# A transformer block on one core: a ring of three PSUM banks for the maxima, two for dense products, a split gelu block, two reciprocal transfers, and a new order of all steps

## What is computed

```python
c_proj = silu(c) @ W_mod + b_mod
shift_a, scale_a, gate_a, shift_m, scale_m, gate_m = split(c_proj, 6)
q, k, v = split(modulate(ln(x), shift_a, scale_a) @ W_qkv + b_qkv, 3)
x = x + gate_a * (softmax(q k^T / 4) v @ W_proj + b_proj)           # self attention
q_c = ln(x) @ W_qc + b_qc
k_c, v_c = split(ln(context) @ W_kvc + b_kvc, 2)
x = x + softmax(q_c k_c^T / 4) v_c @ W_cproj + b_cproj               # cross attention
h = gelu_tanh(modulate(ln(x), shift_m, scale_m) @ W_mlp1 + b_mlp1)
x = x + gate_m * (h @ W_mlp2 + b_mlp2)
```

## Time and profile before

| | |
|---|---|
| Median of three runs | 1634.08 us (1629.98 to 1639.45) |
| The profiled execution | 1633.06 us, span 1631.3 us |
| Mean granted clock of TensorE | 0.958 of full |
| PE busy | 1406.4 us, 86% |
| DVE, ACT, POOL busy | 1145.2 (70%), 1130.6 (69%), 718.4 (44%) |

### The profile page before, as it was taken

How to read it: one execution, slowest core, us unless ns; L and a number is a source line. 1 busy time by engine, 2 the same in 40 slices (tenths; PEclk the granted TensorE clock), 3 DMA queues, 4 the chain that set the end, 5 groups by cost and what they waited for, 6 DMA issues and landing times.

```text
span 1631.3 us, 40543 instructions
## 1 busy us (share of the span) xinstructions
PE 1406.4 (86%) x15090; PEld 918.4 (56%) x15090; DVE 1145.2 (70%) x2477; ACT 1130.6 (69%) x2343; POOL 718.4 (44%) x1005
## 2 busy tenths in 40 slices
PE   3477899989999899999999999999999998988764
PEld 1234466666666666666665666666666566655433
DVE  4657877777887777777788777777778877765411
ACT  3144687877777777787777778777777777776541
POOL 2232345454455445445445544544544544543222
PEclk8678999999999999999999999999999999999877
DMA  5122333233233233233323333323232323321100
GB/s 157 51 74 74 94 92 90 91 89 95 81 97 92 86 89 96 87 90 90 93 86 96 89 90 90 95 90 88 90 99 81 95 85 90 86 74 59 44 28 20
DMA packets 166118, 138.08 MB, mean 85 GB/s; under 512 B 45921, under 2 KB 156674, under 8 KB 165922
## 3 DMA queue, kind: packets, MB, share of 16 engines
q1 hardware_dynamic: 165922, 135.48, 27.9%
HBM read 56.60 MB, written 9.57 MB: 41 GB/s over the span
## 4 chain that ended last, share of the span: by engine, by line
PE 33%; SPq 20%; ACT 20%; DMA 11%; DVE 8%; issue 5%; POOL 3%; POOLq 0%; ACTq 0%; DVEq 0%
SPq L436 12%; PE o_ps L678 8%; SPq L469 6%; ACT G L835 6%; PE dense_ps L351 5%; PE max_ps L643 4%; PE dense_ps L353 4%; PE dense_ps L352 4%; DMA r_dram_cross<-o_r_cross 4%; DMA o_rb_cross<-r_dram_cross 3%; ACT g_split L789 3%; DVE mx_self L1002 3%; PE exp_ps L660 3%; ACT probs L804 3%; PE dense_ps L585 3%
## 5 line engine op out<-in xcount | busy, mean ns | idle before, releaser
L804 ACT ACTIVATE probs<-exp_ps 128x512 f32<-128x512 f32 x1024 | 558.1, 602 | 247.8 <-PE exp_ps L660 244.6
L1002 DVE TENSOR_REDUCE mx_cross<-max_ps 128x2 f32<-128x512 f32 x512 | 328.4, 683 | 202.6 <-PE max_ps L643 198.4
L1002 DVE TENSOR_REDUCE mx_self<-max_ps 128x2 f32<-128x512 f32 x512 | 329.0, 684 | 62.6 <-PE max_ps L643 59.3
L1110 POOL TENSOR_TENSOR o_n_self<-o_n_self,o_rb_self 128x512 f32<-128x512 f32 x32 | 40.6, 1269 | 267.1 <-DMA o_rb_self<-r_dram_self 267.1
L1143 POOL TENSOR_TENSOR g_split<-G,g_split 128x512 f16<-128x512 f32 x128 | 144.7, 1156 | 28.2 <-ACT g_split L789 26.6
L660 PE MATMUL exp_ps<-q_stack_cross,k_stack_cross 50*128 50x256 f16 x1024 | 100.7, 274 | 63.8 <-ACT probs L804 55.4
L351 PE MATMUL dense_ps<-mlp_hi,g_split 128*128 128x256 f16 x512 | 141.9, 277 | 6.4 <-POOL g_split L1143 3.9
L678 PE MATMUL o_ps<-probs,V_cross 128*32 128x256 f32 x2048 | 141.9, 396 | 0.6 <-ACT o_sb_cross L812 0.6
L351 PE MATMUL dense_ps<-xt,mlp_hi 128*128 128x256 f16 x512 | 140.7, 275 | 1.9 <-DVE xt L964 1.9
L678 PE MATMUL o_ps<-probs,V_self 128*32 128x256 f32 x2048 | 142.2, 397 | 0.0
L352 PE MATMUL dense_ps<-mlp_lo,g_split 128*128 128x256 f16 x512 | 140.7, 275 | 0.0
(11 more groups left out here) (212 smaller groups left out, 3351.3 us busy)
## 6 DMA issues: line engine op xcount, KB each, us to landing
q_stack_self<-split_q SPq DMA_DIRECT2D x192, 64.0 KB, 2.6
k_stack_self<-split_k SPq DMA_DIRECT2D x192, 64.0 KB, 2.5
k_stack_cross<-split_kc SPq DMA_DIRECT2D x192, 64.0 KB, 2.6
q_stack_cross<-split_qc SPq DMA_DIRECT2D x192, 64.0 KB, 2.6
X<-in_x SPq DMA_DIRECT2D x32, 256.0 KB, 2.8
Ctx<-in_ctx SPq DMA_DIRECT2D x32, 256.0 KB, 3.0
rows_a<-rows_a_dram SPq DMA_DIRECT2D x32, 256.0 KB, 4.1
o_n_self<-o_sb_self SPq DMA_DIRECT2D x64, 128.0 KB, 3.0
```

The costliest lines, as they stand in the source:

```text
L804: nc.scalar.activation(probs[:, (t + ab) % 8], exp_ps[:, ab], ACT.Exp).then_inc(exp_taken[kind], 1)
L1002: nc.vector.tensor_reduce(mx[kind][:, :, ab, t // 2], max_ps[:, ab].rearrange("p (q k) -> p q k", q=2), AX_X, ALU.max).then_inc(max_taken[ ...
```

## The change

- The maxima get a ring of three banks. A MAX pair waits until all tiles but the last one of the pairs before have been reduced. The dense units have two banks left.
- The gelu block has the four pairs of gelus only. The copies to float16 become four steps `g_hi_0` to `g_hi_3` with slots of their own. A gelu of one element on `gelu_primer` stands ahead of the wait for `mlp1_0`.
- `r_fetch` reads the reciprocals back in two DMAs of 64 partitions instead of eight of 16. `o_sb` and `r_dram` are laid out to fit.
- All steps have new slots, and EXP begins in slot 8 instead of 6. The order is now computed in `Timeline` from absolute slots, with the same lags and the same order in a slot.

```diff
 PLAN = {
-    "load_x": (-1, 0, 0), "ln1": (-1, 0, 4), "norm1": (-1, 0, 6), "t1": (-1, 0, 8), "t1_hi": (-1, 0, 9),
-    "t1_lo": (-1, 0, 10), "q": (-1, 1, 1), "q_hi": (-1, 1, 3), "q_lo": (-1, 1, 4), "stack_q": (-1, 1, 8),
-    "k": (-1, 1, 6), "k_hi": (-1, 1, 6), "k_lo": (-1, 1, 8), "stack_k": (-1, 1, 10), "v": (0, 0, 7),
-    "v_hi": (0, 0, 8), "split_self": (0, 0, 15), "m_self": (0, 1, 0), "m_copy_self": (0, 1, 0),
-    "o_gather_self": (1, 0, 13), "o_recip_self": (1, 0, 13), "r_out_self": (1, 0, 14), "r_back_self": (1, 0, 14),
-    "o_norm_self": (1, 0, 14), "o_hi_self": (1, 1, 4), "o_lo_self": (1, 1, 7), "rows_a": (0, 1, 7),
-    "xr": (0, 1, 12), "proj": (1, 1, 9), "x2": (1, 1, 11), "x2_add": (1, 1, 11), "ln2": (1, 1, 13),
-    "norm2": (1, 1, 14), "t2": (2, 0, 1), "t2_hi": (2, 0, 1), "t2_lo": (2, 0, 2), "qc": (2, 0, 5),
-    "qc_hi": (2, 0, 5), "qc_lo": (2, 0, 6), "stack_qc": (2, 0, 8), "xc": (3, 1, 10), "load_c": (0, 0, 14),
-    "lnc": (0, 0, 15), "normc": (0, 1, 7), "tc": (1, 0, 14), "tc_hi": (1, 0, 14), "tc_lo": (1, 0, 15),
-    "kc": (1, 1, 3), "kc_hi": (1, 1, 7), "kc_lo": (1, 1, 9), "stack_kc": (2, 0, 5), "vc": (2, 0, 10),
-    "vc_hi": (2, 0, 11), "split_cross": (3, 0, 0), "m_cross": (3, 0, 0), "m_copy_cross": (3, 0, 2),
-    "o_gather_cross": (3, 1, 10), "o_recip_cross": (3, 1, 13), "r_out_cross": (3, 1, 13),
-    "r_back_cross": (4, 0, 1), "o_norm_cross": (4, 0, 1), "o_hi_cross": (4, 0, 4), "o_lo_cross": (4, 0, 4),
-    "cproj": (4, 0, 6), "x3": (4, 0, 7), "ln3": (4, 0, 9), "norm3": (4, 0, 12), "rows_b": (3, 1, 4),
-    "t3": (4, 0, 13), "t3_hi": (4, 0, 13), "t3_lo": (4, 0, 14), "xm": (4, 0, 13), "mlp1_0": (4, 1, 0),
-    "mlp1_1": (4, 1, 1), "mlp1_2": (4, 1, 1), "mlp1_3": (4, 1, 1), "gelu": (4, 1, 0), "g_lo_0": (4, 1, 6),
-    "g_lo_1": (4, 1, 6), "g_lo_2": (4, 1, 6), "g_lo_3": (4, 1, 7), "mlp2_0": (4, 1, 10), "mlp2_1": (4, 1, 12),
-    "mlp2_2": (4, 1, 14), "mlp2_3": (5, 0, 2), "y": (5, 0, 4), "y_add": (5, 0, 4), "store": (5, 1, 3),
+    "max_self": (0, 0, 0), "exp_self": (0, 1, 8), "max_cross": (2, 1, 0), "exp_cross": (3, 0, 8),
+    "load_x": (-1, 0, 4), "ln1": (-1, 0, 9), "norm1": (-1, 0, 11), "t1": (-1, 0, 13), "t1_hi": (-1, 0, 13),
+    "t1_lo": (-1, 0, 13), "q": (-1, 0, 15), "q_hi": (-1, 0, 15), "q_lo": (-1, 1, 0), "stack_q": (-1, 1, 6),
+    "k": (-1, 1, 0), "k_hi": (-1, 1, 0), "k_lo": (-1, 1, 5), "stack_k": (-1, 1, 9), "v": (0, 0, 12),
+    "v_hi": (0, 0, 12), "split_self": (0, 1, 0), "m_self": (0, 1, 3), "m_copy_self": (0, 1, 3),
+    "o_gather_self": (1, 0, 11), "o_recip_self": (1, 0, 12), "r_out_self": (1, 0, 13), "r_back_self": (1, 0, 14),
+    "o_norm_self": (1, 1, 6), "o_hi_self": (1, 1, 6), "o_lo_self": (1, 1, 10), "rows_a": (0, 1, 13),
+    "xr": (1, 0, 3), "proj": (1, 1, 13), "x2": (1, 1, 13), "x2_add": (1, 1, 15), "ln2": (1, 1, 15),
+    "norm2": (2, 0, 8), "t2": (2, 0, 8), "t2_hi": (2, 0, 8), "t2_lo": (2, 0, 8), "qc": (2, 0, 11),
+    "qc_hi": (2, 0, 11), "qc_lo": (2, 0, 11), "stack_qc": (2, 0, 12), "xc": (3, 1, 1), "load_c": (0, 1, 1),
+    "lnc": (1, 0, 10), "normc": (1, 1, 1), "tc": (1, 1, 9), "tc_hi": (1, 1, 9), "tc_lo": (1, 1, 9),
+    "kc": (2, 0, 1), "kc_hi": (2, 0, 4), "kc_lo": (2, 0, 7), "stack_kc": (2, 0, 11), "vc": (2, 0, 14),
+    "vc_hi": (2, 0, 15), "split_cross": (2, 1, 15), "m_cross": (2, 1, 15), "m_copy_cross": (3, 0, 1),
+    "o_gather_cross": (3, 1, 10), "o_recip_cross": (3, 1, 14), "r_out_cross": (3, 1, 15),
+    "r_back_cross": (4, 0, 6), "o_norm_cross": (4, 0, 9), "o_hi_cross": (4, 0, 10), "o_lo_cross": (4, 0, 10),
+    "cproj": (4, 0, 13), "x3": (4, 0, 13), "ln3": (4, 0, 13), "norm3": (4, 1, 3), "rows_b": (4, 0, 0),
+    "t3": (4, 1, 4), "t3_hi": (4, 1, 5), "t3_lo": (4, 1, 8), "xm": (5, 0, 11), "mlp1_0": (4, 1, 10),
+    "mlp1_1": (4, 1, 10), "mlp1_2": (4, 1, 10), "mlp1_3": (4, 1, 10), "gelu": (4, 1, 10), "g_hi_0": (4, 1, 10),
+    "g_hi_1": (4, 1, 13), "g_hi_2": (4, 1, 15), "g_hi_3": (5, 0, 1), "g_lo_0": (4, 1, 12), "g_lo_1": (5, 0, 0),
+    "g_lo_2": (5, 0, 1), "g_lo_3": (5, 0, 1), "mlp2_0": (5, 0, 5), "mlp2_1": (5, 0, 8), "mlp2_2": (5, 0, 9),
+    "mlp2_3": (5, 0, 10), "y": (5, 0, 10), "y_add": (5, 0, 12), "store": (5, 1, 14),
 }
 
 BANK = {
-    "m_self": 2, "m_cross": 0, "qc": 2, "cproj": 0, "tc": 0, "kc": 1, "t3": 1, "mlp1_0": 1, "mlp1_1": 0,
-    "mlp1_2": 2, "mlp1_3": 1, "vc": 1, "t1": 0, "proj": 0, "mlp2": 1, "q": 0, "k": 2, "v": 1, "t2": 2,
+    "m_self": 1, "m_cross": 1, "qc": 0, "cproj": 0, "tc": 0, "kc": 0, "t3": 1, "mlp1_0": 0, "mlp1_1": 1,
+    "mlp1_2": 0, "mlp1_3": 1, "vc": 0, "t1": 1, "proj": 0, "mlp2": 1, "q": 1, "k": 0, "v": 1, "t2": 0,
 }
 
-DENSE = {n: BANK[n] for n in sorted(BANK, key=lambda n: PLAN["mlp2_0" if n == "mlp2" else n][1:])}
-MAX_LAG = {"self": 0, "cross": 2}
-EXP_LAG = {"self": 0, "cross": 3}
-EXP_START = 6
+AHEAD = {}
+
+PE_ORDER = ("m_self", "m_cross", "qc", "cproj", "tc", "kc", "t3", "mlp1_0", "mlp1_1", "mlp1_2", "mlp1_3", "vc", "t1",
+            "proj", "mlp2", "q", "k", "v", "t2")
 AV_AFTER = 6
+MAX_BANKS = 3
...
+def moment(step, n):
+    lag, half, slot = PLAN[step]
+    return ((n + lag) * 2 + half) * TILES + slot - AHEAD.get(n, {}).get(step, 0)
+class Timeline:
+    def __init__(self, batches, kinds):
+        self.steps, self.max, self.exp, self.av = {}, {}, {}, {}
+        for n in range(batches):
+            b = Batch(n)
+            for kind in kinds:
+                for t in range(0, TILES, 2):
+                    self.max[moment(f"max_{kind}", n) + t] = (kind, b, t)
+                    self.exp[moment(f"exp_{kind}", n) + t] = (kind, b, t)
+                for g in range(4):
+                    self.av[moment(f"exp_{kind}", n) + AV_AFTER + 4 * g] = (kind, b, g)
+            for step in PLAN:
+                if step[:4] not in ("max_", "exp_"):
+                    self.steps[step, moment(step, n)] = b
+        assert len(self.steps) == batches * (len(PLAN) - 2 * len(kinds))
+        assert len(self.max) == len(self.exp) == batches * len(kinds) * TILES // 2
+        def predecessors(turns):
+            turns = [t[1:] for t in sorted(turns)]
+            return dict(zip(turns[1:], turns))
+        every = [(kind, n) for kind in kinds for n in range(batches)]
+        self.max_before = predecessors((moment(f"max_{k}", n), k, n) for k, n in every)
+        self.max_at = {t[1:]: i for i, t in enumerate(sorted((moment(f"max_{k}", n), k, n) for k, n in every))}
+        self.exp_before = predecessors((moment(f"exp_{k}", n), k, n) for k, n in every)
+        self.tenant_before = {}
+        for bank in set(BANK.values()):
+            self.tenant_before.update({unit[1:]: before[1:] for unit, before in predecessors(
+                (moment("mlp2_0" if u == "mlp2" else u, n), i, u, n)
+                for i, u in enumerate(PE_ORDER) if BANK[u] == bank for n in range(batches)).items()})
+        self.first = min(at for _, at in self.steps)
+        self.last = max(max(at for _, at in self.steps), max(self.av))
...
-        max_ps, exp_ps, o_ps, dense_ps = psum("max_ps", 2), psum("exp_ps", 2), psum("o_ps", 1), psum("dense_ps", 3)
+        max_ps, exp_ps, o_ps, dense_ps = psum("max_ps", MAX_BANKS), psum("exp_ps", 2), psum("o_ps", 1), psum("dense_ps", 2)
...
+        def max_bank(kind, b, tile):
+
+            return (line.max_at[kind, b.n] * TILES + tile) % MAX_BANKS
...
             def r_fetch(b, kind):
                 sp_wait(r_out[kind][b.u], dmas(b, 1))
                 sp_wait(o_mult[kind], b.n)
                 for g in range(2):
-                    for j in range(4):
-                        src = r_dram[kind][b.u, j, :, g]
-                        (i_step, i_n), (e_step, e_n) = [tuple(v) for v in src.ap]
-                        nc.sync.dma_start(o_rb[kind][64 * g + HD * j:64 * g + HD * j + HD],
-                                          bass.AP(tensor=src.tensor, offset=src.offset,
-                                                  ap=[[0, HD], [i_step, i_n], [e_step, e_n]])).then_inc(o_rb_in[kind][b.u], 16)
+                    rows = r_dram[kind][b.u, :, g]
+                    (j_step, j_n), (e_step, e_n) = [tuple(v) for v in rows.ap]
+                    nc.sync.dma_start(o_rb[kind][64 * g:64 * g + 64],
+                                      bass.AP(tensor=rows.tensor, offset=rows.offset,
+                                              ap=[[j_step, j_n], [0, HD], [e_step, e_n]])).then_inc(o_rb_in[kind][b.u], 16)
...
+            def tenant(b, unit):
+
+                if (prev := line.tenant_before.get((unit, b.n))):
+                    pe.wait_ge(taken[prev[0]], prev[1] + 1)
+                return dense_ps[:, BANK[unit]]
+
...
-                    if (prev := previous(it, max_order, MAX_LAG, kind)):
-                        pe.wait_ge(max_taken[prev[0]], prev[1].n * TILES + TILES)
+                    if (prev := line.max_before.get((kind, b.n))):
+                        pe.wait_ge(max_taken[prev[0]], prev[1] * TILES + TILES - 1)
                 else:
```

(31 more changed lines are left out.)

621 lines of the change are left out of this document (277 added, 344 removed).

## The result

The changed kernel takes 1626.59 us (median; 1621.13 to 1633.67) against 1633.69 for the kernel before on the same chip: ratio 0.9958, 95% interval 0.9942 to 0.9974. It is faster by 0.4%, where 2.9% was forecast: inside the range, far from the value. The prediction called anything within 8 us no change and gave it a chance of 0.08.

The account below looks back on a forecast made before the run. TensorE was taken to bound the steady stretch, busy 92%, with ACT and DVE waits; a loop bound the drain. Steady -16, filling -4 and drain -27 sum to -47 us from 1634.08: 1587 us, range 1552 to 1632.

Parts of the forecast that it names:

- filling, first gelu load: Filling: cheaper MAX pairs save 4 us, while the new plan puts gelu 12.8 us later in its iteration.
- steady stretch: 27 iterations between gelu loads 1 and 28: period from 45.4 to 44.8 us, a gain of 16 us.
- loads 28 to 32: Drain: gelu no longer holds up the next batch's exponents, so four iterations take 126 us instead of 167.6.
- end behind it: After the last gelu load: stays near 23 us, with 2 us lost for the last batch, whose copies follow all gelus.
- the ring: PE's waits on maxima banks: 1.0 us gained an iteration; in the filling a MAX pair about 0.6 cheaper, -4 us altogether.
- the landing of the reciprocals: Two wide read-back DMAs: landing taken as 3 us, 4.3 from first issue to POOL's product, covered by the plan.
- rival D: Wide reciprocal transfer or `stack_qc` lands late, blocking ACT and DVE: 1684 us, or 1641 with one late by 2; chance 0.11.
- rival E: The drain's loop stays shut by in-order queues and the steady gain is nil: 1630 us; chance 0.08.
- `mlp1_2` with two dense banks: Dense unit `mlp1_2` must wait for the gelu of unit 0 to free its bank: cost 0.24 us an iteration.
- The wait behind the gelu block: PE waiting for exponents (EXPs6) after the gelu block: 1.8 us an iteration, where it waited 1.6 before.
- New waits of tight exponents: Closely spaced exponents wait for ACT: EXPc14 0.43, EXPs0 0.15, EXPs2 0.61 us, together 1.2 an iteration.
- The prediction's own sign of being wrong: Drain: gelu loads still 40 us apart in the profile after, instead of 29 to 33, would show the forecast wrong.

Follow-up runs that it names:

- e7: e1 with PE waiting for all earlier maxima tiles to be taken, as two banks would force, so the third bank goes unused; 1633.8 us.
- e1: Changed kernel with each reciprocal row read back in a DMA of its own, eight for a head set instead of two; 1600.8 us.
- e3: Changed kernel with four reciprocal DMAs of two rows and 32 partitions instead of two of four rows and 64; 1725.6 us.
- e6: Changed kernel with one reciprocal DMA of eight rows, `r_dram` laid out head set first and denominators gathered in two DMAs; 1601.6 us.
- e4: Changed kernel with the two cross reciprocal DMAs issued earlier, `r_back_cross` at slot (4,0,0) instead of (4,0,6); 1607.4 us.
- e5: Changed kernel with `load_x` moved from right ahead of the cross reciprocal DMA pair to right behind it; 1606.0 us.
- e11: e7 with two banks for the maxima and a third dense bank that `mlp1_2` alone uses; 1625.1 us.
- e10: e1 without the small gelu that loads the gelu table early, ahead of the wait for `mlp1_0`; 1632.2 us.
- e12: e1 with the last copy left in the gelu block, `g_hi_0`, moved behind the first exponents after the block; 1674.8 us.
- e14: e12 with `x2` and `o_recip_cross` placed behind the split of the cross maxima and `ln2` at (2,0,1); 1641.8 us.
- e13: e12 with POOL's subtraction `g_lo_0` moved to (5,0,0), behind `x2_add`; 1630.8 us.
- e9: e1 with copies `g_hi_1` to `g_hi_3` back in the gelu block, ahead of the exponent table's load; 1686.7 us.

## Why the prediction was right or wrong

**Against the profiled execution** (-46.8 forecast, -12.3 measured) the terms stand so:

| term | forecast | measured |
|---|---|---|
| filling, first gelu load (-4, and 12.8 later by plan) | +8.8 | +8.8 |
| steady stretch | -16 | -4.8 |
| loads 28 to 32 | -41.6 | -19.4 |
| end behind it | +2 | +3.1 |

(For the last batch, which needs no load, the start of its first gelu at 1596.13 is taken.)

The first row agrees by luck. By e7 the ring is worth 7.2 us of filling, not 4, so the rest of the plan puts the first load some 16 us later, not 12.8. In the last row the prediction has the end before "near 23"; by the earlier trace rows it is 19.8, and 22.9 after.

**The steady stretch** failed in one term, the landing of the reciprocals. The prediction took a landing of 3 us, so 4.3 from first issue to product; 7.3 is the median (7.87 in the rows shown), a landing of 6. The prediction named the row that was nearest, 3.9 for a broadcast of 256 KB, and the rule that spoke against its 3, and then took a value between the rows, by size; by e1, e3 and e6 size is not what orders the landings. With the landing on time (e1, e4, e5, e6) the period is 44.54 to 44.57; 44.8 was forecast, 16.2 us in 27 iterations, and it would have been 22. (The steady sum leaves out the 0.1 that the prediction had booked for the other dense units.) The point from which rival D decides, a landing of 6 us, was about right: with 7.3 from issue to product the changed kernel loses 0.65 us an iteration, with 6.6 (e5) nothing. Its price, 38 us for one product late by 2, was too high: the cross product is 1.3 us later than in e1, and the profile 20 us longer. So the time lies near that of rival E (1630), but the cause is that of D; the prediction had the mechanism of its loss among its rivals and priced it out of the range.

**Ring, banks, early load.** 1.0 an iteration for the ring: 0.78 by e7, and 7.2 us of filling where 4 was taken. 0.24 for `mlp1_2` with two dense banks: 0.30 by e11. The wait behind the gelu block: 1.8 by start times (1.82 in the sum), 1.56 idle measured, 1.73 by start times (MAX at 1082.12, EXP at 1084.08 in e1, less 0.23). New waits of tight exponents, by start times, 0.43, 0.15 and 0.61: 0.49, 0.24 and 0.53 in e1, of which 0.32, 0 and 0.37 are idle. These steps were right. The gains do not add up, though: without the ring alone (e7) or the early load alone (e10) the whole gain of e1 is gone. No run takes the new order of steps back, so its own share is not known.

**The drain** failed by the size of one iteration. I took 33, 32, 32 and 29 us for the four and measured 42.9, 42.1, 32.8 and 30.4. The pieces of one drain iteration were listed as if it held the cross half alone. Two windows of the changed kernel:

```profile
1448.00:1491.00 43.00, 36.24 (x382) 21.89 (x381) 20.32 (x46) 30.60 (x63) 19.77 (x26) 0.96 0.21 64
1491.00:1533.00 42.00, 33.29 (x300) 21.42 (x301) 20.60 (x42) 21.93 (x45) 14.96 (x19) 0.88 0.16 46
```

PE alone is busy for 36.2 and 33.3 us: between load 28 and 29 the self exponents of the last batch, and up to load 30 most of its cross maxima and the projections for them, are still to be done. Work was missing from the sum, not waits. The prediction's own sign of being wrong, loads still 40 us apart, came for these two. Only the third and fourth are of the kind that was costed. The late transfer adds to it: with eight DMAs the first two are 41.6 and 38.0. That the loop is open fits the third interval, 46.4 before and 32.8 now. This account of the drain rests on traces alone; no run changed the drain by itself.

**The rest.** The profile's difference is -12.3 and that of the medians -7.1; the profiled execution of the changed kernel (1621.13) is the fastest of its 20, which makes the 5 between them. The profile of e1 (span 1598.7) is 14 us above the forecast's sum: 19.4 in the drain and the end (167.2 from load 28 on, where 147.8 was forecast), 1.1 in the filling, less the 6 us by which its steady stretch is better.

**Not seen at all** was that small steps away from the new plan make it slower. That PE's wait behind the block couldn't be turned into a gain by 0.5 us less of it (e12 to e14) has two reasons that no step of the prediction had: DVE is held up by POOL, and PE's clock falls (e12, e13; in e14 it stays).

Best of all measured, by the ratios, are e1 and e6, 1.7 to 1.8% below the kernel before; e6 gets there with one DMA.

## What to carry to other kernels

Merging DMAs saves issue time, but look at the outermost count of the merged pattern before its size, and at what is issued right beside it: the same edit gained 9 us in one plan and cost 26 in the other. When an in-order queue holds an operation that waits, price what stands behind it (here `Y`, which needed nothing of it). Count the work of a drain iteration by what the batches in flight still owe, from the plan, before any wait.

## What the runs showed of the hardware

- Four DMAs with an outermost count of two deliver the same 256 KB 3.6 us later than one DMA with an outermost count of eight (8.01 and 4.37 us from first issue to product, e3 and e6).
- A transfer of 256 KB that lands in 2.8 us takes 5.9 when it is issued right behind the two-DMA pair (e5); the pair itself is then 0.7 us quicker.
- DVE operations of 0.12 and 0.19 us take 1.00 to 1.20 beside POOL's, and end within 0.05 us of them (e12). In e13 the first takes 0.12 in 19 iterations of one execution and 1.13 in 8, with POOL's start at the same 0.07 us ahead of it.
- PE's granted clock, 1.00 with one wait of 1.56 in an iteration (e1), fell to 0.50 (1.2 GHz) behind waits of 1.04 and 1.63 with 1.4 us of work between them in 20 of 27 iterations (e12), and stayed there mostly for some 3 us of full work. It fell behind one wait of 3.12 in 24 of 27 (e9), and behind waits of 2.0 to 3.1 in some of the iterations of e3.
